# The mean of squares of the second norm: one TensorE product over a sum made by GpSimd, with v's products around it

## The reference, cut to what matters

```python
def _rmsnorm(x):
    return x * jax.lax.rsqrt(jnp.mean(x * x, axis=-1, keepdims=True) + EPS)

x = x + a_alpha * _attention(_ada_rmsnorm(x, t, attn_gamma_w, attn_beta_w), W_q, W_k, W_v, W_o)
x = x + f_alpha * _swiglu(_ada_rmsnorm(x, t, ffn_gamma_w, ffn_beta_w), gate_w, hidden_w, out_w, out_b)
# then: rmsnorm -> up projection, val * gelu(gate), 8-bit rounding -> ternary down projection
# then: an adapter whose weights depend on the batch, then a layer norm -> out
```

## Time and profile before

| | |
|---|---|
| median of three runs | 986.26 us (983.16 to 986.62) |
| the profiled execution | 990.35 us, of it 988.0 us from first to last instruction |
| PE busy | 941.6 us (95%) |
| DVE busy | 737.2 us (75%) |
| ACT busy | 577.5 us (58%) |
| POOL busy | 259.6 us (26%) |
| length of one pass of the loop | 55.3 us |

### The profile page before, as it was taken

How to read it: one execution, slowest core, us unless ns; L and a number is a source line. 1 busy time by engine, 2 the same in 40 slices (tenths; PEclk the granted TensorE clock), 3 DMA queues, 4 the chain that set the end, 5 groups by cost and what they waited for, 6 DMA issues and landing times.

```text
span 988.0 us, 21368 instructions
## 1 busy us (share of the span) xinstructions
PE 941.6 (95%) x6772; PEld 786.3 (80%) x6772; DVE 737.2 (75%) x1700; ACT 577.5 (58%) x1197; POOL 259.6 (26%) x343
## 2 busy tenths in 40 slices
PE   8676999999999999999999999999999999998997
PEld 7344669888888979788888979798888979796876
DVE  5853568786877878787878778887878787885746
ACT  3263664857666574847666574747566564746542
POOL 2232602222231322222222323222222313211220
PEclk8797999999999999999999999999999999999999
DMA  7898752130404022130404031130404031120000
GB/s 220 271 290 303 254 210 65 46 107 3 150 1 139 11 91 59 44 106 1 150 1 142 9 101 50 52 98 7 143 1 145 6 113 37 60 81 2 22 17 16
DMA packets 75776, 89.43 MB, mean 91 GB/s; under 512 B 16528, under 2 KB 62112, under 8 KB 73184
## 3 DMA queue, kind: packets, MB, share of 16 engines
q1 hardware_dynamic: 70960, 72.24, 24.0%
q0 software_dynamic: 1440, 9.18, 2.8%
q10 hardware_dynamic: 3344, 7.60, 2.1%
HBM read 63.14 MB, written 25.31 MB: 90 GB/s over the span
## 4 chain that ended last, share of the span: by engine, by line
PE 81%; DMA 6%; DVE 5%; issue 2%; SPq 2%; ACT 2%; POOL 1%; DVEq 0%; ACTq 0%; POOLq 0%
PE bank L803 18%; PE bank L867 16%; PE bank L817 8%; PE bank L762 8%; PE bank L772 6%; PE bank L729 6%; PE bank L780 3%; PE bank L884 3%; DMA k_stack<-k_dram 2%; PE bank L709 2%; DMA hyper<-w_hyper 2%; PE bank L904 2%; DMA q_stack<-few_rows 1%; PE bank L877 1%; PE bank L898 1%
## 5 line engine op out<-in xcount | busy, mean ns | idle before, releaser
L597 POOL TENSOR_TENSOR act_lo<-act_f,act_hi 128x256 fp32r<-128x256 f32 x120 | 88.2, 735 | 361.8 <-ACT act_hi L1269 361.8
L1538 DVE TENSOR_REDUCE neg_max<-bank 128x2 f32<-128x512 f32 x256 | 161.8, 680 | 2.1 <-PE bank L729 2.1
L1216 ACT ACTIVATE probs<-bank 128x512 f32<-128x512 f32 x256 | 135.3, 602 | 29.1 <-PE bank L762 17.9
L1305 ACT ACTIVATE gelu_g<-bank,r 128x256 f32<-128x256 f32 x128 | 60.6, 474 | 86.9 <-PE bank L867 85.6
L1263 ACT ACTIVATE silu_g<-bank 128x256 f32<-128x256 f32 x128 | 49.1, 384 | 102.8 <-PE bank L803 102.3
L803 PE MATMUL bank<-h_hi,gh_hi 128*128 128x256 f32 x512 | 104.1, 285 | 0.0
L1618 DVE TENSOR_TENSOR act_f<-bank,silu_g 128x256 f32<-128x256 f32 x128 | 53.6, 419 | 67.6 <-ACT silu_g L1263 67.5
L803 PE MATMUL bank<-h_lo,gh_hi 128*128 128x256 f32 x512 | 103.6, 284 | 0.0
L803 PE MATMUL bank<-h_hi,gh_lo 128*128 128x256 f32 x512 | 103.4, 284 | 0.0
L1269 ACT ACTIVATE act_hi<-act_f 128x256 fp32r<-128x256 f32 x128 | 53.4, 417 | 74.7 <-DVE act_f L1618 72.0
L803 PEld LDWEIGHTS bank<-h_hi,gh_hi 128*128 128x128 f32 x512 | 83.4, 190 | 9.2 <-issue 5.1
(11 more groups left out here) (236 smaller groups left out, 2091.5 us busy)
## 6 DMA issues: line engine op xcount, KB each, us to landing
q_stack<-q_dram SPq DMA_DIRECT2D x96, 128.0 KB
k_stack<-k_dram SPq DMA_DIRECT2D x90, 128.0 KB
q_dram<-probs SPq DMA_DIRECT2D x16, 512.0 KB, 2.8
k_dram<-probs SPq DMA_DIRECT2D x16, 512.0 KB, 2.8
hyper<-w_hyper POOLq DMA_DIRECT2D x8, 1024.0 KB, 10.2
hyper<-w_hyper SPq DMA_DIRECT2D x8, 1024.0 KB, 5.3
x_res<-xT SPq DMA_DIRECT2D x16, 256.0 KB, 2.8
out<-xc SPq DMA_DIRECT2D x15, 256.0 KB, 2.4
```

The source lines that it names most:

```text
L597: pool.tensor_tensor(act_lo[:, c % 3, :], act_f[:, c % 2, :], act_hi[:, c % 3, :].bitcast(F32), ALU.subtract).then_inc(g_lo.sem, 1)
L1216: act.activation(probs[:, h % SLOTS], halves(SCORE_BANKS[h]), ACT.Exp, scale=float(H / D) ** 0.5).then_inc(s_exp.sem, 1)
L1305: act.activation(gelu_g[:, n % 2, :], halves(7 - n % 2)[:, 1, :], ACT.Gelu, scale=r3[:, t:t + 1])\
L1538: dve.tensor_reduce(neg_max[:, qt, pair, :], halves(n % 3), AX_X, ALU.max, negate=True).then_inc(max_red.sem, 1)
```

## The change

GpSimd gets a new step `sum_f`, which waits for both squares of the second norm and adds chunk 1 to chunk 0 of `h2` in place. It stands between `sum_square_x` and `layer_out`. TensorE's `norm_f` waits for that sum (`n2_sum`) and then does one product instead of two. For the first batch the old form stays.

TensorE's order becomes: first v group, `norm_f`, up groups 0 and 1, second v group, up groups 2 to 7. ScalarE's `copy_v` moves behind gelu 2, because the second v group now comes after up group 1.

```diff
+                def sum_f(b):
+
+                    pool.wait_ge(n2_act.sem, n2_act.at(b, DC))
+                    pool.tensor_tensor(h2[:, 0, :], h2[:, 0, :], h2[:, 1, :], ALU.add).then_inc(n2_sum.sem, 1)
...
                     if g:
                         sum_square_x(g)
+                    if a and f:
+                        sum_f(a)
+                    if g:
                         layer_out(g)
...
                 def norm_f(b):
                     if b.follows():
                         pe.wait_ge(g_dve.sem, g_dve.at(b, back=1))
+                        pe.wait_ge(n2_sum.sem, n2_sum.at(b, back=1))
+                        mean_of_sum(bank[4][:, 0:T], h2[:, 0, :]).then_inc(n2_pe.sem, 1)
+                        return
                     for c in range(DC):
...
-                    if a:
+                    if starts(a):
                         norm_f(a)
                     if nxt:
                         project_v(nxt, 0)
+                    if a and f:
+                        norm_f(a)
+                    if starts(a):
                         project_v(nxt, 1)
...
                         for n in range(8):
                             up(f, n)
+                            if nxt and n == 1:
+                                project_v(nxt, 1)
...
-                        if nxt and n == 1:
+                        if nxt and n == 2:
                             copy_v(nxt)
```

More of the change, by code:

```diff
@@ L262, in build @@
         den_act, o_dve, o_act = sem("den_act", 4), sem("o_dve", 16), sem("o_act", 2)
-        n1_sum, n3_sum, n4_sum = sem("n1_sum"), sem("n3_sum"), sem("n4_sum", 2)
+        n1_sum, n2_sum, n3_sum, n4_sum = sem("n1_sum"), sem("n2_sum"), sem("n3_sum"), sem("n4_sum", 2)
         wo_mm, x1_dve, x1_bias = sem("wo_mm", DC), sem("x1_dve", 2), sem("x1_bias", DC)
```

## The result

The changed kernel takes 1000.01 us (median of 4 runs, 996.24 to 1002.37), the kernel before 986.09 (4 runs, 983.16 to 986.62). The ratio is 1.013, with a 95% interval of 1.0106 to 1.0154: slower by 13.9 us. Forecast were 995.8 us in a range of 988.0 to 999.5. The direction was right; the time lies 4.2 us above the forecast and 0.5 above the range.

A forecast was written before the change was run, and what follows sets the result against it. VectorE's queue was taken to set up group 2, though TensorE is busy 95%. Per pass 0.49 + 0.22 - 0.06 = +0.65 us, 9.1 for batches 1 to 14, with batch 15 9.5: 986.3 + 9.5 = 995.8 us, range 988 to 999.5.

The forecast's parts named there:

- The saved product: TensorE ahead of up group 2: one product less, 0.43 us a pass, worth nothing because VectorE's queue sets that place.
- Rival B: TensorE is the bound and the product is simply saved: 6.5 us less in all, 979.8 us; chance 0.05.
- C: Rival: copies cost nothing and no collision, 0.3 us in all, 986.6 us; chance 0.06.
- The new wait: TensorE waits for GpSimd's sum ahead of the second norm's mean: 0.02 us at up group 2 if unhindered.
- rival A: No collision between GpSimd's add and VectorE's L1648: 988.8 us; chance 0.18.
- The collision: GpSimd's add and VectorE's pair L1648 take turns at SBUF: up group 2 0.49 us late a pass; chance 0.68.
- the dearer of the orders: Bound of the collision where GpSimd gets in first: VectorE 0.58 us late, 0.74 a pass, 997.2 us.
- The second v group ... fills idle time there; it adds nothing: TensorE between up 1 and up 2: its 0.70 us fill idle time, adding nothing; its waits are long met.
- copy_v: ScalarE's copies behind gelu 2 delay gated product 3: up group 5 loses 0.22 us, later groups take back 0.06.
- rival D: The new standstill ahead of the up groups lowers TensorE's clock, adding only to the slower side; chance 0.03.
- The 0.4 that I gave to batch 15: Last full pass, without v or copies: only the collision, shortened to an estimated 0.4 us.

The follow-up runs named there:

- e6: Changed kernel with VectorE's pair L1664 ahead of L1545, second v group again ahead of up group 0, copy_v again behind gelu 1: 990.48 us, ratio 1.0032.
- e8: e6 and e7 together (one product with GpSimd's sum, Newton instructions spread): 990.28 us, ratio 1.0034 against the kernel before.
- e1: Changed kernel with two products again and no GpSimd add, new places of second v group and copies kept: 992.36 us, ratio 1.0061.
- e3: Changed kernel with only copy_v back behind gelu 1: 998.39 us, ratio 1.0120 against the kernel before.
- e2: Changed kernel with second v group back ahead of up group 0 and copy_v behind gelu 1, add kept: 994.53 us, ratio 1.0077.
- e4: Kernel before plus a GpSimd add of 128 x 232 that nobody waits for, started by the second square: 991.90 us, ratio 1.0052.
- e7: Kernel before with the second norm's Newton instructions and what hangs on them spread behind gated products 0 to 4: 985.50 us, ratio 0.9974.
- e5: Changed kernel with VectorE's pair L1664 moved ahead of L1545: 992.02 us, ratio 1.0051 against the kernel before.

## Why the prediction was right in direction, and where it failed

1. **The saved product, worth nothing: right.** e6 and e8 have it without collision and without the new places, and are slower by 0.28 and 0.27 a pass. Rival B (979.8) is out, and so is C (no change): both collision and copies show.
2. **The new wait, 0.02 unhindered: too cheap, though it didn't show in the full passes.** The mean came nearly as priced: from the square's end to the logarithm 1.66 us (526.51 to 528.17), 0.48 more than before, 0.42 forecast (527.64 - 527.22). Gelu 0 came 0.30 later, not 0.21, and I had let the gated product follow gelu's end at once, when it follows 0.19 behind (e8: 526.35 to 526.54). Gated product 0 would thus come at 526.04 + 3.91 + 0.48 + 0.19 = 530.62 instead of 530.44, 0.18 late. In the changed kernel the collision's 0.55 covers it. In e6 and e8, where the collision is gone, it comes out with the 0.12 of the add's wait for its turn: 0.30 by this sum, +0.28 and +0.27 measured. Had rival A been true, it would have cost this too. Batch 15 shows it in the changed kernel itself: no v stands there, VectorE is ahead, and its gated product 0 idles 0.41 us for gelu 0. From the start of the second square to the load of up group 2 it takes 5.47 us (919.86 to 925.33), before 4.92 (914.03 to 918.95): 0.55 later.
3. **The collision: right, in the dearer of the orders.** I gave VectorE the first turn and priced 0.49. GpSimd got in first, for which the bounds had 0.58; 0.55 was measured at gated product 0, and 0.56 a pass as the difference to e1. This order costs 0.06 a pass more than forecast, some 0.8 us of the 4.2. Rival A is out.
4. **"The second v group ... fills idle time there; it adds nothing": this step failed.** It adds 0.27 a pass at up group 2 (0.82 - 0.55) and 0.24 between e3 (+0.80) and e2 (+0.56), which have the copies alike: 3.4 to 3.8 us over 14 passes, the bulk of the miss. I had asked what up group 2 waits for, and taken up group 0 to run at once behind the norm's product ("norm 527.31 to 527.74, up 0 and 1 to 530.52"). The order of the change lists `n3_dve` among its waits, VectorE's row scale, and I did not look up when that ends: 0.28 us ahead of up 0 before, covered by v's second group (e1). The collision, which I did price, made VectorE 0.55 later just there too. TensorE then stood still 0.59 us ahead of up 0 with v's second group queued behind the wait, and did it afterwards, when gated product 0 was nearly there. The same work in its old place would have filled that hole: in e2 it does.
5. **copy_v: right.** From up 2 to up 5 a pass loses 0.20 (4.14 us before, 4.34 after, each with 0.10 added to the start of a pair behind a late load), 0.22 was forecast; later groups take back 0.05, 0.06 was forecast. e3 confirms it with 0.17.
6. **The clock (rival D): out.** Over the twelve passes from 203.42 to 870.17 the granted clock is 1.00, as it was before (207.50 to 860.02); the new stall of 0.6 us in each did not lower it. The mean of the whole execution is 0.983 after and 0.980 before. The low stretch in batch 15 of the profile before was there in those of e1, e2, e3, e4 and e7 too. The profiles of e5, e6, e8 and of the changed kernel do not have it there; those of e5 and e8 have a shorter one later (0.97 on average over 930 to 980). One profile of each kernel can't tell whether it belongs to the kernel or to the execution; by the rows of batch 15 it is worth 1.5 us (from the end of batch 14's up groups to the second square 42.69 us before, 41.18 after). Whether the changed kernel wins that back in every execution stays open.

The sum as it should have been: 0.55 + 0.27 + 0.15 = 0.97, over 14 passes 13.6, and 0.5 for batch 15: 986.1 + 14.1 = 1000.2 (998.7 if the 1.5 us of point 6 belong to the kernel). The 0.4 that I gave to batch 15 came out near by luck: there is no late VectorE in that pass, since it had the turn; the wait for the sum costs there instead (point 2).

The Trainium skill, page "SBUF — State Buffer", section "SBUF: two separate sides", says that VectorE and GpSimd share a port pair under an exclusive lock, held for a whole instruction by the one that starts first, and that a VectorE operation with two SBUF inputs takes part. The trace agrees on the lock and on the kind of operation (e4: 0.869 instead of 0.480; L1545 with a PSUM input unhindered at 0.683). On who starts first it agrees only loosely: VectorE's L1664 is stamped 526.57, GpSimd's add 526.59, and GpSimd had the turn. The measurement decides: two starts this close can't be told apart by their stamps.

## What to carry to other kernels

Work that one engine leaves to another isn't priced by its duration alone: look at what the helping engine stands beside, since two SBUF readers on VectorE and GpSimd take turns and the later one stands still for nearly all of the other's instruction. Before an instruction group is moved out of a gap, ask of every instruction that moves up in its place which waits it has, those too that never showed, because the group's own duration was their cover. And where two engines end within 0.2 us of each other at one place, as VectorE's queue and gelu 0 do here, relieving one earns only that difference (e7: 0.13 us a pass), and delaying the other costs all of the delay but that difference (e8: gelu 0 comes 0.41 us later, the pass is 0.27 longer).

## What the runs showed of the hardware

- TensorE's granted clock fell to the lower of its two levels (0.50) behind a standstill of 2.02 us in one execution, and stayed at 1.00 behind one of 2.01 us in another.
- A VectorE instruction stamped 0.02 us earlier than GpSimd's lost its turn to it: 1.03 us instead of 0.48. In e5, where VectorE was in the middle of its second instruction, GpSimd waited 0.12 for it and VectorE lost nothing; so too in batch 15 of the changed kernel.
- The price of a turn is what is left of the other's instruction less 0.14 to 0.18 us: VectorE lost 0.55 to an add of 0.735 and 0.39 to one of 0.574; in e5 the add lost 0.12 to a pair that ended 0.26 behind its stamp (525.87, and 525.26 + 0.87).
- GpSimd's add of 128 x 256 took 0.735 us and that of 128 x 232 0.574 (least 0.572, median 0.574): 9% fewer columns, 22% less time. Why, these runs don't tell; the two also differ in their operands (the shorter one reads one tile twice).
